# Attention values in key halves over two PSUM banks, turns behind scores, low parts of the sums on GpSimd

## The chip, the cores and the metric

The kernel runs on one core of a Trainium2 chip. The metric is device time in microseconds; the median of three runs of the kernel before is 915.81 us (915.44 to 916.83).

## What is computed

A decoder layer on x (2 x 2048 rows of 512 features): linear self-attention, cross-attention to 154 context rows a batch with 16 heads of 32, and a gated feed-forward, each followed by a layer norm.

```python
x = _layernorm(x + _L0_attn_ref(x, w_qkv, b_qkv, w_o, b_o))          # no softmax: folds into one 512x512 matrix a batch
x = _layernorm(x + _L0_xattn_ref(x, ctx_1024, ctx_1024, mask, ...))
#   scores = q @ k.T / sqrt(32); masked; softmax over 154 keys; out = attn @ v; out @ W_o.T + b_o
x = _layernorm(x + _L0_ffn_ref(x, W_r, W_k, W_v, mu_r, mu_k))
#   xr, xk = blends of x and the row before; sigmoid(xr @ W_r.T) * (relu(xk @ W_k.T) ** 2 @ W_v.T)
```

## The kernel before, in words

Everything is f32. A large product is made of three passes of f32r parts (`three_pass`, L91): high x high, high x low, low x high. So each operand is split: ScalarE writes the high part, VectorE or GpSimd subtracts it to get the low part. The small products of attention and the transposes ("turns") are plain f32.

`prologue` (L117) sums x into a Gram matrix for each batch, makes the keys (`kt`) and values of the context and places the values in the halves and pieces that attention wants (`placements`, DMAs from `v_raw` to `v_first` and `v_rest`), and folds batch 0's self-attention into the matrix `m`.

`layers` (L610) goes over 16 groups of 256 rows (`GT`), two tiles t = 0, 1 of 128 rows. The order of each engine's work is written out by hand, in one program for each engine, and overlapped: in round n TensorE does cross-attention of group n, the first product and q of group a = n + 1, the output product and x2 turns of f = n - 1, and the feed-forward of e = n - 2. Rounds 0 and 1 also fold batch 1. LAST = 15. Semaphores (`Flag`) tie the engines; a `wait_ge` holds everything behind it on its engine.

Cross-attention of a group goes in four head groups g of four heads:
- `scores(n, g)` (L1641): q times keys, 32-row positions, into four banks.
- `masked_min` (VectorE, L1150) adds the mask and takes the row minimum; `exponentials` (ScalarE, L813); `weigh` (GpSimd, L1431) divides by the row sum: `row_inv`, then the keys 128 to 153 into `rest`, then the first 128 into `weight`, whose columns are ordered by key half and head.
- `transposes(n, g, t)` (L1654) turns the weights into the bank `t_bank`; `take_turned` and `take_rest` (ScalarE) copy them to `prob_t`.
- `values(n, g)` (L1671): 24 products, each 64 rows of the array by 32 columns, for three pieces (keys 0 to 63, 64 to 127, the rest), two t and four heads. All pieces of one head and t are summed in PSUM in one row half (`side_of`), in columns 256 to 383 of the two banks `rv_bank` and `t_bank`.
- `o_high` (ScalarE, L833) and `o_low` (VectorE, L1165) read that sum from PSUM and write `o_t_hi` and `o_t_lo`. The next `transposes` waits for `ot_lo`, since it writes a bank that they read; so does the second x2 turn (L1718). `o_product` (L1690), one round later, waits for all four.

x1 turns (`x1_turn`, L1618) need the normalised x1 and a free dense bank; x2 turns go into `t_bank`. `x1t_high` (ScalarE) and `x1t_low` (VectorE) split what is turned. `store` and the loads of x and masks stand in SP's queue.

## Time and profile before

| | |
|---|---|
| median of 3 runs | 915.81 us |
| the profiled execution | 914.96 us, of which the span of instructions is 912.9 us |
| TensorE busy | 896.7 us, 98% |
| VectorE busy | 695.6 us, 76% |
| ScalarE busy | 556.5 us, 61% |
| GpSimd busy | 521.8 us, 57% |
| TensorE's granted clock | 0.998 of full |

Each time in the rows further down is from this one execution. PE is TensorE, DVE VectorE, ACT ScalarE, POOL GpSimd. A row of the timeline gives the start, the length and the instruction; what stands in brackets behind it is the idle time of the engine before it and what ended that. Instructions of one engine overlap a little at their ends, so a row can start before the one ahead has ended.

### The profile page before, as it was taken

What the parts mean: (1) busy time and instruction counts of PE and PEld (TensorE: products, weight loads), DVE (VectorE), ACT (ScalarE), POOL (GpSimd) and SP (SyncE); (2) the same over time, 40 slices, a digit from 0 to 9 for tenths busy, and PEclk for the clock granted to TensorE, in tenths of its full rate; (3) what the DMA queues carried; (4) which work ended last, traced back from release to release, by engine and by line L of the source; (5) the groups of instructions that cost most, each with busy time, mean ns of one, the idle gap of its engine ahead of it and who ended that gap; (6) DMA issues with size and microseconds to landing.
All of it is one profiled execution on the core that took longest, in us unless ns stands there. A gap on an engine that the chain in (4) does not pass through costs nothing.

```text
span 912.9 us, 23290 instructions
## 1 busy us (share of the span) xinstructions
PE 896.7 (98%) x8774; PEld 749.0 (82%) x8774; DVE 695.6 (76%) x1994; ACT 556.5 (61%) x1667; POOL 521.8 (57%) x505
## 2 busy tenths in 40 slices
PE   8999999999999999999999999999999999999997
PEld 7867766787788888888878888888888888888886
DVE  6688566578877878787877878787877777787775
ACT  7555236858675756575856666666665757575631
POOL 1045015759666666666675757566676767665420
PEclk9999999999999999999999999999999999999999
DMA  8792020113000001012101010101010100100001
GB/s 296 245 271 58 24 94 2 43 36 136 9 25 31 25 25 31 24 32 82 32 24 32 24 32 25 32 25 32 25 32 24 31 26 12 44 2 24 2 24 46
DMA packets 32332, 46.54 MB, mean 51 GB/s; under 512 B 3806, under 2 KB 16606, under 8 KB 32094
## 3 DMA queue, kind: packets, MB, share of 16 engines
q1 hardware_dynamic: 28622, 37.99, 12.8%
q10 hardware_dynamic: 3600, 7.08, 2.3%
q8 instruction: 70, 1.15, 0.5%
q14 instruction: 40, 0.33, 0.1%
HBM read 34.10 MB, written 9.70 MB: 48 GB/s over the span
## 4 chain that ended last, share of the span: by engine, by line
PE 75%; DVE 4%; POOL 4%; issue 4%; ACT 1%; POOLq 0%; ACTq 0%
PE dense L92 19%; PE dense L94 17%; PE dense L93 17%; PE turned L1664 5%; PE turned L1686 5%; PE scores L1650 4%; PE dense L1540 2%; PE turned L1668 1%; PE turned L1540 1%; POOL row_inv L1442 1%; POOL weight L1450 1%; PE scores L1546 1%; DVE mix_k_raw L1204 1%; PE dense L1557 0%; POOL prob_rest L1449 0%
## 5 line engine op out<-in xcount | busy, mean ns | idle before, releaser
L1442 POOL TENSOR_TENSOR row_inv<-row_sum,minus_one 128x4 f32<-128x4 f32 x128 | 152.6, 1192 | 190.1 <-ACT prob L818 190.0
L818 ACT ACTIVATE prob<-prob,row_min 128x154 f32<-128x154 f32 x512 | 209.6, 416 | 39.8 <-DVE row_min L1160 39.8
L1450 POOL TENSOR_TENSOR weight<-prob,row_inv 128x512 f32<-128x512 f32 x128 | 148.0, 1156 | 0.0
L1160 DVE CUSTOM_DVE_ANT_0 prob<-scores,mask_add 128x154 f32<-128x154 f32 x512 | 127.8, 312 | 4.0 <-PE scores L1650 3.7
L826 ACT ACTIVATE prob_t<-turned 128x512 f32<-128x512 f32 x128 | 76.0, 594 | 84.6 <-PE turned L1664 83.8
L818 ACT ACTIVATION_READ_ACCUMULATOR prob<-prob,row_min 128x1 f32 x512 | 98.3, 192 | 0.0
L1664 PE MATMUL turned<-ident,weight 128*128 128x128 f32 x512 | 76.9, 272 | 3.4 <-DVE o_t_lo L1167 3.0
L1664 PEld LDWEIGHTS turned<-ident,weight 128*128 128x128 f32 x512 | 61.2, 139 | 17.9 <-issue 6.3
L92 PE MATMUL dense<-mix_k_hi,ffn_wk_hi 128*128 128x256 f32 x256 | 75.3, 294 | 0.0
L92 PE MATMUL dense<-xt_hi,cross_wq_hi 128*128 128x256 f32 x256 | 75.2, 294 | 0.0
L94 PE MATMUL dense<-mix_k_hi,ffn_wk_lo 128*128 128x256 f32 x256 | 72.3, 283 | 0.0
L93 PE MATMUL dense<-mix_k_lo,ffn_wk_hi 128*128 128x256 f32 x256 | 72.3, 283 | 0.0
L94 PE MATMUL dense<-xt_hi,cross_wq_lo 128*128 128x256 f32 x256 | 72.3, 283 | 0.0
L93 PE MATMUL dense<-xt_lo,cross_wq_hi 128*128 128x256 f32 x256 | 72.3, 282 | 0.0
L837 ACT ACTIVATE o_t_hi<-turned 128x256 fp32r<-128x256 f32 x64 | 24.3, 380 | 64.7 <-PE turned L1686 64.0
L1460 POOL TENSOR_TENSOR x<-x,cross_bo_row 128x1024 f32<-128x1024 f32 x16 | 38.6, 2412 | 40.8 <-PE dense L1540 40.8
L1128 DVE TENSOR_SCALAR x<-x,moments,rstd 128x512 f32<-128x512 f32 x64 | 32.1, 544 | 35.1 <-POOL rstd L1429 35.1
L1449 POOL TENSOR_TENSOR prob_rest<-prob,row_inv 128x104 f32<-128x104 f32 x128 | 51.5, 402 | 10.0
L1454 POOL TENSOR_TENSOR mix_r_lo<-mix_r_raw,mix_r_hi 128x1024 fp32r<-128x1024 f32 x16 | 42.2, 2636 | 24.9 <-ACT mix_r_hi L867 24.9
L92 PE MATMUL dense<-m_hi,xt_hi 128*128 128x512 f32 x128 | 52.3, 408 | 1.4 <-DVE x L1173 1.1
L92 PE MATMUL dense<-cross_wo_hi,o_t_hi 128*128 128x512 f32 x128 | 53.1, 415 | 0.0
L92 PE MATMUL dense<-ffn_wv_hi,k_act_hi 128*128 128x512 f32 (+1 forms) x124 | 52.2, 421 | 0.0
(276 smaller groups left out, 2684.7 us busy)
## 6 DMA issues: line engine op xcount, KB each, us to landing
x_rows<-x_rows SPq DMA_DIRECT2D x32, 256.0 KB, 4.6
xt_raw<-x_cols SPq DMA_DIRECT2D x16, 512.0 KB, 3.8
out<-gate_then_y SPq DMA_DIRECT2D x15, 512.0 KB, 2.8
mask_in<-mask SPq DMA_DIRECT2D x16, 154.0 KB, 2.3
cross_wv<-cross_wv SPq DMA_DIRECT2D x2, 512.0 KB, 6.6
cross_wk<-cross_wk SPq DMA_DIRECT2D x1, 1024.0 KB, 9.3
self_wv<-self_wv ACTq DMA_DIRECT2D x1, 1024.0 KB, 7.3
self_wk<-self_wk ACTq DMA_DIRECT2D x1, 1024.0 KB, 9.6
```

The lines of the kernel that those rows point to most:

```text
L92: pe.matmul(out, sta[0], mov[0], start=first, stop=False, skip_group_check=True)
L93: pe.matmul(out, sta[0], mov[1], start=False, stop=False, skip_group_check=True)
L94: return pe.matmul(out, sta[1], mov[0], start=False, stop=last, skip_group_check=True)
L818: m = act.activation(keys, keys, ACT.Exp, bias=row_min[:, buf, t, h:h + 1], scale=-1.0, accum_out=row_sum[:, buf, t, h:h + 1])
L826: act.activation(pt[:, 0:HPG, t * P:(t + 1) * P], t_bank[:].rearrange("p (c n) -> p c n", c=HPG), ACT.Copy).then_inc(*t_out.up)
L1160: m = dve.tensor_tensor_reduce(exp_slot(n, u)[:, i * CTX:(i + 1) * CTX], s_bank[:, h, t * CTX:(t + 1) * CTX], mask_add[n % 2][:, t, :], -S ...
L1442: pool.tensor_tensor(row_inv[:, buf, t, :], row_sum[:, buf, t, :], minus_one[:], ALU.pow).then_inc(*p_inv.up)
L1449: pool.tensor_tensor(after, late, inv_late, ALU.mult)
L1450: pool.tensor_tensor(first, early, inv_early, ALU.mult).then_inc(*p_norm.up)
L1454: pool.tensor_tensor(mix["r"][1][:], mixed["r"][:], f32(mix["r"][0][:]), ALU.subtract).then_inc(*mix_lo["r"].up)
L1664: m = pe.transpose(t_bank[:, i * P:(i + 1) * P], weight_slot(n, u)[:, i * P:(i + 1) * P], ident[:])
L1686: m = pe.matmul(value[h * DK:(h + 1) * DK, t, :], sta, pt[rows, block, t * P:(t + 1) * P], start=(piece == 0), stop=(piece == PIECES), ski ...
```

## The change

- `values`: 8 products of 64 x 32 positions with 256 moving columns (both t at once) for the first 128 keys, half of the keys in each row half of the array, and 8 of 128 columns for the rest. Row half 0 sums into `rv_bank`, row half 1 into `t_bank`, columns 256 to 511. The weights keep the order of heads (`place_of`), so `v_first` has one copy of each row in place of two.
- The two partial sums are added by VectorE (`o_take`, a reduce over two values) into `o_t_raw` in SBUF. `o_high` reads that. `o_low` reads it too, on GpSimd in the rounds and on VectorE in the last round. `transposes` and the second x2 turn wait for `ot_sum`, `o_product` for `ot_lo` as before.
- `prob0` and `prob1` hold both tiles of a head group and are weighed in place; `masked_min` waits for no `p_norm` and `weigh` for no `t_mm`. The difference of the blends has a tile of its own. There is one `mask_in`, so `load_mask(n)` waits for `mask_ok(n - 1)`.
- Order on TensorE: the first turn of g = 1 and of g = 3 stands directly behind `scores`; x2's second turn stands ahead of x1's; products are split less. The other engines' orders follow; ScalarE does `exponentials(a, 0, ...)` ahead of `take_turned(n, 3, 1)`.
- The prologue has fewer placements and its `take_sums(1)` does not wait for them.

```diff
 def place_of(h, t):
-    return h // SIDES * SIDES + side_of(h, t)
+    return (h + t * SIDES) % HPG
...
-    rest_t, value = rv_bank[:, 0:GT], psum[1][:, :, GT:GT + P]
+    rest_t, value = rv_bank[:, 0:GT], psum[1][:, :, GT:2 * GT]
...
             def o_high(n, g):
-                act.wait_ge(*pv_mm.at(n, g + 1))
-                if n:
-                    act.wait_ge(*o_mm.at(n - 1))
-                act.activation(by_t(ot_hi[:, g, :]), value, ACT.Copy).then_inc(*ot_hi_ok.up)
+                act.wait_ge(*ot_sum.at(n, g + 1))
+                act.activation(ot_hi[:, g, :], ot_raw[:, g, :], ACT.Copy).then_inc(*ot_hi_ok.up)
...
+            def o_take(n, g):
+                dve.wait_ge(*pv_mm.at(n, g + 1))
+                if n:
+                    dve.wait_ge(*o_mm.at(n - 1))
+                dve.tensor_reduce(ot_raw[:, g, :], value.rearrange("p s n -> p n s"), mybir.AxisListType.X, ALU.add).then_inc(*ot_sum.up)
...
+            def o_low(n, g):
+                pool.wait_ge(*ot_hi_ok.at(n, g + 1))
+                pool.tensor_tensor(ot_lo[:, g, :], ot_raw[:, g, :], f32(ot_hi[:, g, :]), ALU.subtract).then_inc(*ot_lo_ok.up)
...
                 elif n + g:
-                    pe.wait_ge(*ot_lo_ok.at(n, g))
+                    pe.wait_ge(*ot_sum.at(n, g))
...
-                for piece in range(PIECES + 1):
-                    for t in range(TPG):
-                        for h in range(HPG):
-                            rows = slice(side_of(h, t) * SIDE_ROWS, (side_of(h, t) + 1) * SIDE_ROWS)
...
+                for side in range(SIDES):
+                    rows = slice(side * SIDE_ROWS, (side + 1) * SIDE_ROWS)
+                    for h in range(HPG):
+                        cols = slice((g * HPG + h) * DK, (g * HPG + h + 1) * DK)
+                        pe.matmul(value[h * DK:(h + 1) * DK, side, :], v_first[rows, b, cols], pt[rows, h, :],
+                                  start=True, stop=False, skip_group_check=True)
+                for t in range(TPG):
+                    for h in range(HPG):
+                        side = place_of(h, t) // SIDES
+                        rows = slice(side * SIDE_ROWS, (side + 1) * SIDE_ROWS)
+                        m = pe.matmul(value[h * DK:(h + 1) * DK, side, t * P:(t + 1) * P],
+                                      v_rest[rows, b, g, h * DK:(h + 1) * DK], pt[rows, HPG, t * P:(t + 1) * P],
+                                      start=False, stop=True, skip_group_check=True)
...
                 scores(n, 2)
+                transposes(n, 1, 0)
                 y_product(a, 1)
-                transposes(n, 1, 0)
+                transposes(n, 1, 1)
                 r_product(e, 0)
-                transposes(n, 1, 1)
...
                 scores(n, 3)
+                x2_turn(f, 1)
                 x1_turn(a, 1)
-                x2_turn(f, 1)
...
                 scores(a, 0)
+                transposes(n, 3, 0)
                 v_product(e, 0)
-                transposes(n, 3, 0)
-                v_product(e, 1, early)
                 transposes(n, 3, 1)
-                v_product(e, 1, late_half)
+                v_product(e, 1)
                 values(n, 3)
...
                 if live(e - 1):
                     scale(3, e - 1)
+                if live(f):
+                    o_low(f, 3)
                 if a >= 2:
                     x_low(a)
```

TensorE behind `scores(n, 2)` of a settled round, before (`weight` is what the turn of g = 1 reads; its row stands 12 products further on):

```order
L1650 MATMUL scores<-kt,q 128x154 [waits s_min,q_out]
L1650 MATMUL scores<-kt,q 128x154 x7
L92 MATMUL dense<-m_hi,xt_hi 128x512 [waits o_sum]
L93 MATMUL dense<-m_lo,xt_hi 128x512
L94 MATMUL dense<-m_hi,xt_lo 128x512
```

and now:

```order
L1656 MATMUL scores<-kt,q 128x154 [waits s_min,q_out]
L1656 MATMUL scores<-kt,q 128x154 x7
L1671 MATMUL turned<-ident,prob_91 128x128 [waits ot_sum,p_norm]
L1671 MATMUL turned<-ident,prob_91 128x128 x3
L90 MATMUL dense<-m_hi,xt_hi 128x512 [waits o_sum]
```

The turn has moved ahead of the whole y product and waits for `ot_sum`.

TensorE behind `scores(n, 3)`, before (x_1_88 is x1, x_1_98 is x2):

```order
L1650 MATMUL scores<-kt,q 128x154 [waits s_min,q_out]
L1650 MATMUL scores<-kt,q 128x154 x7
L1540 MATMUL dense<-ident,x_1_88 128x128 [waits r_out,ln1]
L1540 MATMUL dense<-ident,x_1_88 128x128 x3
L1540 MATMUL turned<-ident,x_1_98 128x128 [waits ot_lo,ln2]
```

and now (x_1_99 is x2):

```order
L1656 MATMUL scores<-kt,q 128x154 [waits s_min,q_out]
L1656 MATMUL scores<-kt,q 128x154 x7
L1545 MATMUL turned<-ident,x_1_99 128x128 [waits ot_sum,ln2]
L1545 MATMUL turned<-ident,x_1_99 128x128 x3
L1545 MATMUL dense<-ident,x_1_88 128x128 [waits r_out,ln1]
```

The x2 turn, which waits for the sum of g = 1, is now the first of the two.

GpSimd at the turn from round to round, before (from the second tile of g = 0):

```order
L1442 TENSOR_TENSOR row_inv<-row_sum,minus_one 128x4 [waits p_exp]
L1449 TENSOR_TENSOR prob_rest_92<-prob,row_inv 128x2x2x26 [waits t_mm,rest_mm,p_inv]
L1450 TENSOR_TENSOR weight<-prob,row_inv 128x4x2x64
L1429 TENSOR_TENSOR rstd_1449<-var_1448,neg_half 128x2 [waits ln3,var3]
L1422 TENSOR_TENSOR xt_lo<-xt_raw,xt_hi 128x1024 [waits x_hi_ok]
```

and now:

```order
L1436 TENSOR_TENSOR row_inv<-row_sum,minus_one 128x4 [waits p_exp]
L1441 TENSOR_TENSOR prob_rest_92<-prob_90,row_inv 128x4x26 [waits rest_mm,p_inv]
L1442 TENSOR_TENSOR prob_90<-prob_90,row_inv 128x4x128
L1428 TENSOR_TENSOR rstd_1441<-var_1440,neg_half 128x2 [waits ln3,var3]
L1447 TENSOR_TENSOR o_t_lo<-o_t_raw,o_t_hi 128x256 [waits ot_hi]
L1421 TENSOR_TENSOR xt_lo<-xt_raw,xt_hi 128x1024 [waits x_hi_ok]
```

The low part of g = 3 stands behind two tiles' weights and an `rstd`.

## Rows read from the trace of the kernel before

**Rows 1.** Busy time by stretch: us of each engine (instructions), granted clock, DMA share, GB/s.
```profile
288.50:335.50 47.00, 47.00 (x506) 40.07 (x506) 36.73 (x115) 30.15 (x97) 31.39 (x31) 1.00 0.09 28
```

**Rows 2.** Timeline, VectorE and TensorE, rounds 0 to 2: start, us, instruction, idle before.
```profile
159.53 0.41 DVE L1167 TENSOR_TENSOR o_t_lo<-turned,o_t_hi 128x256 fp32r<-128x256 f32 x1
...
160.09 0.63 PE L1664 MATMUL turned<-ident,weight 128*128 128x128 f32 x4 [2.00 <-DVE o_t_lo L1167]
...
211.71 0.63 PE L1664 MATMUL turned<-ident,weight 128*128 128x128 f32 x4 [0.98 <-DVE o_t_lo L1167]
...
235.11 0.47 PE L92 MATMUL dense<-ffn_wr_hi,mix_r_hi 128*128 128x512 f32 x1 [0.92 <-DVE x L1136]
...
245.43 0.63 PE L1540 MATMUL turned<-ident,x 128*128 128x128 f32 x4 [0.81 <-DVE o_t_lo L1167]
```

**Rows 3.** Timeline of TensorE, round 6, values(6,0) to the turn of g = 1.
```profile
419.34 0.67 PE L1686 MATMUL turned<-prob_t,v_first 64*32 64x128 f32 x32
419.80 0.48 PE L1686 MATMUL turned<-prob_t,v_rest 64*32 64x128 f32 x16
420.21 0.81 PE L1650 MATMUL scores<-kt,q 32*128 32x154 f32 x16
420.94 0.50 PE L92 MATMUL dense<-m_hi,xt_hi 128*128 128x512 f32 x1
...
423.80 0.60 PE L1664 MATMUL turned<-ident,weight 128*128 128x128 f32 x4
```

**Rows 4.** Chain that ended last: start us, us, what.
```profile
118.65 3.43 PE scores L1546 x8
```

**Rows 5.** Groups by line and form: busy us, mean ns; idle before, releaser.
```profile
L1167 DVE TENSOR_TENSOR o_t_lo<-turned,o_t_hi 128x256 fp32r<-128x256 f32 x64 | 27.0, 422 | 23.9 <-ACT o_t_hi L837 23.9
...
L1115 DVE BATCH_NORM_STATS2 stats<-x 128x6 f32<-128x512 f32 x64 | 44.4, 695 | 2.2
...
L1460 POOL TENSOR_TENSOR x<-x,cross_bo_row 128x1024 f32<-128x1024 f32 x16 | 38.6, 2412 | 40.8 <-PE dense L1540 40.8
```

**Rows 6.** Timeline of TensorE, round 6, behind scores(6,3).
```profile
433.00 0.66 PE L1540 MATMUL dense<-ident,x 128*128 128x128 f32 x4
433.49 0.60 PE L1540 MATMUL turned<-ident,x 128*128 128x128 f32 x4
```

**Rows 7.** Timeline of ScalarE, round 6.
```profile
420.33 0.38 ACT L837 ACTIVATE o_t_hi<-turned 128x256 fp32r<-128x256 f32 x1 [4.20 <-PE turned L1686]
...
451.45 0.42 ACT L818 ACTIVATE prob<-prob,row_min 128x154 f32<-128x154 f32 x1
```

**Rows 8.** Timeline of VectorE, round 6.
```profile
420.63 1.00 DVE L1128 TENSOR_SCALAR x<-x,moments,rstd 128x512 f32<-128x512 f32 x2 [1.66 <-POOL rstd L1429]
...
432.18 0.69 DVE L1147 TENSOR_TENSOR xt_lo<-dense,xt_hi 128x512 fp32r<-128x512 f32 x1 [2.90 <-ACT xt_hi L802]
432.80 0.42 DVE L1167 TENSOR_TENSOR o_t_lo<-turned,o_t_hi 128x256 fp32r<-128x256 f32 x1
...
446.27 0.42 DVE L1167 TENSOR_TENSOR o_t_lo<-turned,o_t_hi 128x256 fp32r<-128x256 f32 x1 [2.04 <-ACT o_t_hi L837]
```

**Rows 9.** Timeline of all engines, start of round 6.
```profile
405.19 0.67 PE L1686 MATMUL turned<-prob_t,v_first 64*32 64x128 f32 x32
...
408.10 0.42 DVE L1167 TENSOR_TENSOR o_t_lo<-turned,o_t_hi 128x256 fp32r<-128x256 f32 x1
...
410.13 0.48 PE L92 MATMUL dense<-cross_wo_hi,o_t_hi 128*128 128x512 f32 x1
...
411.46 0.70 POOL L1429 TENSOR_TENSOR rstd<-var,neg_half 128x2 f32<-128x2 f32 x1
...
412.60 3.08 DVE L1128 TENSOR_SCALAR gate_then_y<-gate_then_y,moments,rstd 128x512 f32<-128x512 f32 x2
```

**Rows 10.** Timeline of VectorE and TensorE, last round.
```profile
841.06 0.67 PE L1686 MATMUL turned<-prob_t,v_first 64*32 64x128 f32 x32
...
843.40 0.41 DVE L1167 TENSOR_TENSOR o_t_lo<-turned,o_t_hi 128x256 fp32r<-128x256 f32 x1
```

474 lines of the change are left out of this document (228 added, 246 removed).

## The prediction

> **What bounds the kernel.** I read the busy shares and slices of the page first: TensorE is busy 98% of the span of 912.9 us, at the full granted clock (2.4 GHz) in every slice. The windows say it more sharply [rows 1]: in one round TensorE is busy 47.00 of 47.00 us, VectorE 36.73, ScalarE 30.15, GpSimd 31.39. So in a settled round (one of n = 2 to 14, 47.0 us each) TensorE never waits, and the other engines live in its shadow. TensorE's few waits lie in the rounds before [rows 2], and one of 1.1 us at the turn of the batch. What the change can win is time in which TensorE works; what it can lose is any wait that TensorE has not got now. I went through TensorE's timeline of round 6 with those of VectorE, ScalarE and GpSimd beside it, measuring from the start of each `values` block, called v.
>
> **Values in two banks.** Today a block is 24 products of 128 columns, 48 passes since f32 runs as two: 419.34 to 420.21, 0.87 us [rows 3]. The change makes 8 products of 256 columns and 8 of 128, 32 passes. A full f32 pass of 512 columns takes 3.43/8 = 0.43 us [rows 4], so 0.107 for 128 columns and 0.214 for 256. Eight positions run together, so today 6 x 0.107 = 0.64 us stand in a row, and then 2 x 0.214 + 2 x 0.107 = 0.64: the same. What can shrink is the rest, 0.87 - 0.64 = 0.23. If that is all fixed, nothing is won; if it is per pass, 4 of 6 shares stay and 0.08 is won. I take 0.055, nearer to the second, since the last 16 passes are slow (0.41 us for 16, 0.46 for the 32 before), though part of that is the change of shape to `scores`. 64 blocks: **-3.5 us** (0 to -5). All 32 first passes of today run in 0.46 us, four bursts of 0.115, with both row halves writing one bank. The Trainium skill ("TensorEngine Tiling (Array Packing)", "Gotcha 1: PSUM Pressure") says that different row tiles cannot use one PSUM bank at a time. By it today's halves would take turns, 8 x 0.107 = 0.86 us for those 32, and separate banks would save much more; the trace disagrees, and my sum has no such term.
>
> **The sum out of two banks.** VectorE gets `o_take`, a reduce over 2 x 256 values in PSUM, and gives up `o_low` (0.42). No reduce is in the trace. By its output it would take the 0.42 of `o_t_lo`, by its 512 inputs the 0.69 of `bn_stats` [rows 5]. I take 0.69, since `bn_stats` writes only 6 values and pays for the 512 it reads. That is 0.27 more, 64 times, on an engine with 10 us free a round: nothing by itself. What counts is when it is done, because TensorE's next write to the turned bank waits for it (`ot_sum`).
>
> **Turns behind scores.** The first turn of g = 1 and of g = 3 moves from behind a product (2.86 us, 420.94 to 423.80 [rows 3]) to right behind `scores`. On TensorE itself the first turn behind `scores` takes 0.49 (433.00 to 433.49 [rows 6]), a tenth more than within a product, and a product broken up once less gives nearly that back: 28 places, +0.3 us at most. But the cover is gone. For g = 1 `scores` is over at v + 0.815 + 0.735 = v + 1.55. A reader of the finished sums starts today at 420.33, v + 0.99 [rows 7], so at v + 0.93 with the shorter block; VectorE is idle there (1.66 us before 420.63 [rows 8]) and is done at v + 1.62. From a VectorE end to TensorE's start it is 0.15 (159.94 to 160.09 [rows 2]). The turn starts at v + 1.77: a new wait of 0.22. For g = 3 VectorE is idle too, from 444.23 [rows 8], v + 0.5, and the wait is the same. 2 x 0.22 x 13 rounds: **+5.7 us** (0 if the reduce takes 0.42).
>
> **The dearest place: x2 before x1 behind scores(n,3).** Today the x1 turn goes first (433.00), and the x2 turn, which waits for the sums of g = 1, follows at 433.49 [rows 6], just after `o_t_lo` ends at 433.22 [rows 8]. Now x2 comes first and wants to start at v + 1.55 = 432.95. But on VectorE `o_take(n,1)` still stands behind `x1t_low(a,0)`, which waits for ScalarE and starts at 432.18 [rows 8] whatever the change does. So the reduce starts at 432.80, ends at 433.49, and TensorE goes on at 433.64. A wait of 0.69 in 13 rounds: **+9.0 us** (+5.5 if the reduce takes 0.42). That such a wait reaches TensorE is seen in round 2, where a late `o_t_lo` holds this very turn for 0.81 [rows 2].
>
> **Low parts on GpSimd.** GpSimd adds 1024 values in 2.41 us [rows 5], so 256 in about 0.65, four times a round, out of 15.6 us free. Only the last one has a reader near: `o_product(f,0)` waits for `ot_lo(f,3)`. Today that is done at 408.52 and wanted at 410.13, with v = 405.19, v + 4.94 [rows 9]. Then: VectorE is free of `v_finish` at 408.10, v + 2.91; reduce until 3.60, high part on ScalarE (0.38 [rows 7]) until 4.02, GpSimd until 4.75, TensorE 4.90; wanted 4.88. What stands in GpSimd's queue ahead decides: today `weigh(n,0,1)` ends at 411.46 [rows 9], 1.4 us too late. But the change puts ScalarE's exponentials of the next tile ahead of the last turned copies, about 3.6 us sooner than today's 451.45 [rows 7], and that work of GpSimd's with them, to about v + 2.7. So **0 us** (0 to +0.5 a round). GpSimd's later low parts have over 1 us of slack by the same walk. One thing gets better: the two normalises at 412.60, 3.08 us in place of 1.00 [rows 8, 9] because GpSimd's `xt_lo` runs, find it over sooner.
>
> **Rounds outside the settled ones.** Round 0: the wait of 2.00 at 160.09 goes, since a fold and a product now stand ahead of that turn; but the turn before loses the fold that covered it (2 x 0.43) and has a reduce ahead (0.27 and some tenths): -0.7. Round 1: two waits of 0.2, and the turn at 211.71 (wait 0.98) has half a product, 1.4 us, moved behind it and a reduce ahead: +2.0. Round 2: `y_finish(3,0)` moves up, the wait of 0.92 at 235.11 goes: -0.9 [rows 2]. Last round: no y product stands between `o_product` and `values`, so VectorE comes to `o_take(15,0)` only at 843.40 [rows 10], TensorE goes on at 844.24; with v = 841.06 it wants to at 842.61: +1.4 after some slack. Tail: a reduce in the chain to `o_product(15,0)`, +0.5. Prologue: TensorE waits for no placement, so fewer of them give 0. One mask buffer makes SP wait for the mask, made in the middle of the round; the x load behind it waits for the q product, later, anyway: 0. Together **+2.3 us**.
>
> **Sum.** -3.5 + 0.3 + 5.7 + 9.0 + 0 + 2.3 = +13.8 us. The profiled execution took 914.96 us, 0.85 below the median 915.81 of the runs. 914.96 + 13.8 = 928.8, against the median 929.6. I say **929**.
>
> **Rivals.**
> A, *the reduce costs what it writes*, 0.42: the waits of the turns vanish and x2 keeps 0.42: -3.5 + 0.3 + 0 + 5.5 + 1.2 = +3.5, **919**. For it: `o_t_lo` writes 256 in 0.42. Against: `bn_stats`.
> B, *the block goes by its instructions* (the other side): 48 passes in 0.87 us are 18 ns each, 32 take 0.58, 0.29 saved in 64 blocks: -18.6 in place of -3.5, in all -1; with the cheap reduce too, -12: **903 to 914**. With the waits as worked out it decides from 0.27 saved a block. For it: the slow last 16 passes. Against: bursts of 0.115 are the pass rate of 0.107 already. If the banks did matter, it would be in this case.
> C, *GpSimd is late*: the low part of g = 3 finds GpSimd busy or stretched, by another low part and an `rstd` (0.65 + 0.70 [rows 9]) at most, and `o_product` waits 0.4 to 1.3 us in 13 rounds: +5 to +17, **934 to 946**. For it: the margin worked out is nil, and 3.08 in place of 1.00 [rows 8, 9] shows what the two engines do to each other. Against: 31 of 47 us are in use. The Trainium skill ("SBUF — State Buffer", "Who interferes with whom") says that VectorE, in a two-port mode or with two SBUF inputs, and GpSimd take one shared port pair for a whole instruction and block each other; by it each of the four new GpSimd instructions could hold VectorE up for its length.
> D, *the new order does not bind*: the waits stay under the gain, no change, 915.
>
> **Chances.** Forecast (924 to 934) 0.50; A 0.16; B 0.12; C 0.18; D 0.04. Runs of this kernel can tell 0.2% (1.8 us) from no change. Faster: B and little else, 0.13. Same 0.05. Slower 0.82. The range leaves out B and the far end of C: 916 to 943.
>
> **What would show it.** In a settled round of about 47.9 us, some 1.1 us of TensorE's waits on VectorE's reduce, the longest before the x2 turn; a values block of 0.81; a reduce of 0.69; no wait for GpSimd ahead of `o_product`. A reduce of 0.42, a block under 0.6 or rounds of 47.0 would prove me wrong, each in its own term; rounds over 48.5 with waits at `o_product` would be C.

## The result, and the profile after

The changed kernel takes **950.4 us** (median of 4 runs, 948.85 to 952.64), the kernel before 916.13 beside it: 1.038 times as long (95% interval 1.035 to 1.040), 34 us slower. I had said 929 (916 to 943). The profiled execution took 952.64 us, span 950.9, which is 38.0 more than the 912.9 of before; the comparison of the traces is against these 38. It is the slowest of the four runs of the change, so the traces differ by more than the medians do.

Lines of the page of the changed kernel (the page lists the groups by source line and names what a group waited for): busy times, TensorE's granted clock in 40 slices, the chain that ended last by engine, and the groups of the reduce and of GpSimd's low part (busy us, mean ns, idle before).

```profile
PE 902.5 (95%) x7750; PEld 743.4 (78%) x7750; DVE 721.1 (76%) x2003; ACT 549.0 (58%) x1663; POOL 567.6 (60%) x564
PEclk9999999998999999999999999999999999999999
PE 47%; DVE 24%; issue 9%; POOL 5%; ACT 4%; POOLq 0%; DVEq 0%; ACTq 0%
L1447 POOL TENSOR_TENSOR o_t_lo<-o_t_raw,o_t_hi 128x256 fp32r<-128x256 f32 x59 | 59.0, 999 | 6.3 <-ACT o_t_hi L815 6.3
L1146 DVE TENSOR_REDUCE o_t_raw<-turned 128x256 f32<-128x512 f32 x64 | 43.9, 685 | 23.6 <-PE turned L1694 23.5
```

The reduce is 0.685 as forecast, the low part 1.00 on average where I had worked out 0.65. The third line is the chain that ended last, by engine: a quarter of it now runs over VectorE (the same line before: PE 75%, DVE 4%). Slice 10 has a granted clock below full.

One settled round by the windows view (columns as in [rows 1]). TensorE was busy 47.00 of 47.00 before; now it is busy 47.05 of 48.88, so 1.8 us of every settled round are waits.

```profile
374.14:423.02 48.88, 47.05 (x441) 39.40 (x440) 38.62 (x115) 29.67 (x97) 34.65 (x35) 1.00 0.08 26
```

TensorE's timeline of that round (start, us, instruction, idle before and who ended it), the rows that answer to [rows 3] and [rows 6]:

```profile
374.14 0.66 PE L1688 MATMUL turned<-prob_t,v_first 64*32 64x256 f32 x16
374.60 0.42 PE L1694 MATMUL turned<-prob_t,v_rest 64*32 64x128 f32 x16
374.96 0.81 PE L1656 MATMUL scores<-kt,q 32*128 32x154 f32 x16
...
378.62 0.60 PE L1671 MATMUL turned<-ident,prob 128*128 128x128 f32 x4
379.52 0.50 PE L90 MATMUL dense<-cross_wo_hi,o_t_hi 128*128 128x512 f32 x1 [0.31 <-POOL o_t_lo L1447]
...
389.54 0.81 PE L1656 MATMUL scores<-kt,q 32*128 32x154 f32 x16
390.56 0.63 PE L1671 MATMUL turned<-ident,prob 128*128 128x128 f32 x4 [0.22 <-DVE o_t_raw L1146]
...
401.82 0.81 PE L1656 MATMUL scores<-kt,q 32*128 32x154 f32 x16
403.24 0.63 PE L1545 MATMUL turned<-ident,x 128*128 128x128 f32 x4 [0.61 <-DVE o_t_raw L1146]
...
414.71 0.81 PE L1656 MATMUL scores<-kt,q 32*128 32x154 f32 x16
416.21 0.63 PE L1671 MATMUL turned<-ident,prob 128*128 128x128 f32 x4 [0.69 <-DVE o_t_raw L1146]
```

The values block is 374.14 to 374.96, 0.82 by these rows (0.811 is the median of the 64 blocks, against 0.868 before). Four waits stand in the round. From start to start, with before in brackets: turn to `o_product` 0.91 (0.35), +0.55; `scores` to the turn of g = 1 1.02 (0.74), +0.28; `scores(n,3)` with the x2 and x1 turns 2.24 (1.58), +0.66; `scores(a,0)` to the turn of g = 3 1.50 (0.74), +0.76. Together +2.25. The four blocks give back 0.22. The round is 1.87 longer (48.88 against 47.01), so another 0.16 is given back, which I put down to products that are broken up once less; it is not traced.

Where the 38 us lie, each row from the start of one `values(n,3)` to the next, the last one to the end of TensorE's work:

| stretch | before | after | more |
|---|---|---|---|
| into round 1 | 41.3 | 45.1 | 3.8 |
| into round 2 | 48.9 | 57.6 | 8.8 |
| 12 settled rounds | 565.5 | 586.3 | 20.8 |
| last round | 37.5 | 40.7 | 3.2 |
| behind the last `values` | 39.2 | 40.8 | 1.6 |

Among the 12 is the round at the turn of the batch, 48.31 before with a wait of 1.12 that is gone after; there the change costs only 0.6, which is most of why 20.8 is less than 12 times 1.87.

**Why the sums are late.** VectorE and then GpSimd in the same round:

```profile
375.05 1.41 DVE L1210 SCALAR_TENSOR_TENSOR gate_then_y<-gate_then_y,x 128x512 f32<-128x512 f32 x1
377.52 0.69 DVE L1146 TENSOR_REDUCE o_t_raw<-turned 128x256 f32<-128x512 f32 x1
...
401.80 0.69 DVE L1127 TENSOR_TENSOR xt_lo<-dense,xt_hi 128x512 fp32r<-128x512 f32 x1 [2.76 <-ACT xt_hi L782]
402.41 0.68 DVE L1146 TENSOR_REDUCE o_t_raw<-turned 128x256 f32<-128x512 f32 x1
405.63 2.25 DVE L1173 TENSOR_TENSOR diff<-x_t 128x1024 f32<-128x1024 f32 x1
407.92 2.03 DVE L1183 SCALAR_TENSOR_TENSOR mix_k_raw<-diff,cols,x_t 128x256 f32<-128x256 f32 x4
410.48 2.17 DVE L1183 SCALAR_TENSOR_TENSOR mix_r_raw<-diff,cols,x_t 128x256 f32<-128x256 f32 x4
413.41 2.06 DVE L1189 TENSOR_TENSOR mix_k_lo<-mix_k_raw,mix_k_hi 128x1024 fp32r<-128x1024 f32 x1
415.39 0.68 DVE L1146 TENSOR_REDUCE o_t_raw<-turned 128x256 f32<-128x512 f32 x1
```

```profile
374.87 1.04 POOL L1442 TENSOR_TENSOR prob<-prob,row_inv 128x512 f32<-128x512 f32 x1
378.74 0.73 POOL L1447 TENSOR_TENSOR o_t_lo<-o_t_raw,o_t_hi 128x256 fp32r<-128x256 f32 x1 [0.36 <-ACT o_t_hi L815]
...
404.38 2.41 POOL L1457 TENSOR_TENSOR x<-x,cross_bo_row 128x1024 f32<-128x1024 f32 x1 [3.86 <-PE dense L1545]
406.74 1.74 POOL L1447 TENSOR_TENSOR o_t_lo<-o_t_raw,o_t_hi 128x256 fp32r<-128x256 f32 x1
```

These rows show a relay. The difference starts at 405.63, while GpSimd adds the bias until 406.79; it ends at 407.88, 1.1 us after that. GpSimd's low part, begun at 406.74, ends 0.6 after the difference. Each does most of its own time (1.28 and 0.74 where they hardly meet) only once the other has finished. The same stands at 375.05: the second step of `v_finish` takes 1.41 beside GpSimd's weighing, against 0.69 where nothing meets it (over all 30 the mean went from 0.75 to 1.07). With the turns back behind the products (e2 and e5 below) the weighing ends 0.37 earlier in the round, the step takes 1.05, and `o_product` comes 0.36 sooner after v. The reduce for g = 2 then waits for the whole row of work, until 415.39, though its sums were there at 414.83 or so (0.93 after its values block started, at 413.90).

**Round 2** has the dearest waits. TensorE, GpSimd and ScalarE:

```profile
226.97 0.79 PE L90 MATMUL dense<-cross_wo_hi,o_t_hi 128*128 128x512 f32 x1 [2.88 <-POOL o_t_lo L1447]
255.70 0.63 PE L1545 MATMUL turned<-ident,x 128*128 128x128 f32 x4 [1.97 <-DVE o_t_raw L1146]
```

```profile
222.38 0.41 ACT L815 ACTIVATE o_t_hi<-o_t_raw 128x256 fp32r<-128x256 f32 x1
223.33 1.01 POOL L1436 TENSOR_TENSOR row_inv<-row_sum,minus_one 128x4 f32<-128x4 f32 x1
225.73 1.18 POOL L1447 TENSOR_TENSOR o_t_lo<-o_t_raw,o_t_hi 128x256 fp32r<-128x256 f32 x1
```

The high part is done at 222.8, but in GpSimd's queue the weighing of both tiles (`weigh(2,0,0)` and `weigh(2,0,1)`) stands ahead of the low part. And the wait costs more than itself (windows view; the last three columns are granted clock, DMA share, GB/s):

```profile
224.00:226.00 2.00, 0.09 (x1) 0.00 (x0) 1.05 (x2) 1.75 (x6) 1.92 (x4) 1.00 1.01 385
226.00:228.00 2.00, 1.03 (x3) 0.84 (x4) 0.33 (x1) 1.23 (x7) 2.00 (x2) 0.56 0.11 43
228.00:230.00 2.00, 2.00 (x6) 1.61 (x5) 0.00 (x0) 0.00 (x0) 2.00 (x2) 0.50 0.69 230
230.00:232.00 2.00, 2.00 (x6) 1.52 (x6) 0.00 (x0) 0.00 (x0) 1.56 (x3) 0.50 0.76 294
232.00:234.00 2.00, 2.00 (x12) 1.67 (x11) 1.44 (x3) 0.72 (x2) 0.00 (x0) 0.74 0.00 0
```

After standing nearly idle for two microseconds TensorE is granted half its clock, 1.2 of 2.4 GHz, for some six: the shares missing from 1.00 sum to 0.44 + 0.50 + 0.50 + 0.26 in four windows of 2 us, up to 3.4 us of work lost beside the 2.88 of the wait. The two other long waits of these rounds end likewise: behind the 2.08 before `o_product` in round 1 the windows from 180 to 186 show 0.96, 0.50 and 0.68, 1.7 us lost; behind the 1.97 in round 2 those from 256 to 262 show 0.74, 0.50 and 0.91, 1.7 us. So up to 6.8 of the 38 us are the clock's in this execution.

### The profile page after: what moved, and what is told of

The parts are those of the page before. It is cut to its first block, busy times and chain, and to the rows that moved or that the text cites. A ratio compares the mean times of both kernels' runs of the same rounds, so it can differ in the third digit from the quotient of the medians.

```text
span 950.9 us, 21187 instructions
## 1 busy us (share of the span) xinstructions
PE 902.5 (95%) x7750; PEld 743.4 (78%) x7750; DVE 721.1 (76%) x2003; ACT 549.0 (58%) x1663; POOL 567.6 (60%) x564
## 3 DMA queue, kind: packets, MB, share of 16 engines
q8 instruction: 62, 1.02, 0.4%
## 4 chain that ended last, share of the span: by engine, by line
PE 47%; DVE 24%; issue 9%; POOL 5%; ACT 4%; POOLq 0%; DVEq 0%; ACTq 0%
PE dense L90 13%; PE dense L92 12%; PE dense L91 12%; DVE o_t_raw L1146 4%; PE turned L1671 4%; DVE mix_r_raw L1183 3%; DVE diff L1173 3%; DVE mix_k_lo L1189 3%; DVE gate_then_y L1210 2%; DVE mix_k_raw L1183 2%; DVE stats L1095 2%; ACT xt_hi L782 2%; POOL o_t_lo L1447 1%; PE turned L1545 1%; DVE gate_then_y L1207 1%
## 5 line engine op out<-in xcount | busy, mean ns | idle before, releaser
L1436 POOL TENSOR_TENSOR row_inv<-row_sum,minus_one 128x4 f32<-128x4 f32 x128 | 142.0, 1109 | 138.5 <-ACT prob L798 138.4
L1442 POOL TENSOR_TENSOR prob<-prob,row_inv 128x512 f32<-128x512 f32 x128 | 141.5, 1106 | 0.0
L1671 PE MATMUL turned<-ident,prob 128*128 128x128 f32 x512 | 78.1, 275 | 16.1 <-DVE o_t_raw L1146 15.3
L1671 PEld LDWEIGHTS turned<-ident,prob 128*128 128x128 f32 x512 | 59.7, 141 | 30.5 <-issue 18.8
L815 ACT ACTIVATE o_t_hi<-o_t_raw 128x256 fp32r<-128x256 f32 x64 | 26.5, 414 | 75.8 <-DVE o_t_raw L1146 75.8
L1441 POOL TENSOR_TENSOR prob_rest<-prob,row_inv 128x104 f32<-128x104 f32 x128 | 57.0, 445 | 10.0
L1447 POOL TENSOR_TENSOR o_t_lo<-o_t_raw,o_t_hi 128x256 fp32r<-128x256 f32 x59 | 59.0, 999 | 6.3 <-ACT o_t_hi L815 6.3
L1146 DVE TENSOR_REDUCE o_t_raw<-turned 128x256 f32<-128x512 f32 x64 | 43.9, 685 | 23.6 <-PE turned L1694 23.5
L1428 POOL TENSOR_TENSOR rstd<-var,neg_half 128x2 f32<-128x2 f32 x47 | 32.7, 696 | 47.6 <-DVE var L1102 44.6
L1451 POOL TENSOR_TENSOR mix_r_lo<-mix_r_raw,mix_r_hi 128x1024 fp32r<-128x1024 f32 x16 | 45.4, 2836 | 22.5 <-ACT mix_r_hi L845 22.5
```

The costliest lines, as they stand in the source:

```text
L1146: dve.tensor_reduce(ot_raw[:, g, :], value.rearrange("p s n -> p n s"), mybir.AxisListType.X, ALU.add).then_inc(*ot_sum.up)
L1436: pool.tensor_tensor(row_inv[:, buf, t, :], row_sum[:, buf, t, :], minus_one[:], ALU.pow).then_inc(*p_inv.up)
L1441: pool.tensor_tensor(after, keys[:, :, P:CTX], inv.broadcast_to([P, HPG, CTX - P]), ALU.mult)
L1442: pool.tensor_tensor(keys[:, :, 0:P], keys[:, :, 0:P], inv.broadcast_to([P, HPG, P]), ALU.mult).then_inc(*p_norm.up)
L1447: pool.tensor_tensor(ot_lo[:, g, :], ot_raw[:, g, :], f32(ot_hi[:, g, :]), ALU.subtract).then_inc(*ot_lo_ok.up)
L1671: m = pe.transpose(t_bank[:, h * P:(h + 1) * P], prob[g % 2][:, t, i * CTX:i * CTX + P], ident[:])
```

## The experiments

"The change" below is the changed kernel whole; each experiment starts from it unless said otherwise.

### e1: x1 turn first again

```diff
                 scores(n, 3)
-                x2_turn(f, 1)
                 x1_turn(a, 1)
+                x2_turn(f, 1)
```

(ScalarE's two copies are exchanged likewise; rounds 2 to 14, as in e2 and e5.)

> The changed kernel with one pair of turns exchanged in the rounds 2 to 14: behind scores(n,3) the x1 turn goes first again, then the x2 turn. In the changed kernel the x2 turn stands 0.61 us idle there in every settled round, until VectorE's reduce of g = 1 ends. Theory (the wait is for the reduce, and 0.46 us of other work fits into it): the wait shrinks to about 0.2, the settled round goes from 48.84 to 48.4, and the kernel from 950.4 to about 945. Rival (the wait is given back at the next place, since VectorE sets the pace of the round): round stays 48.8, kernel stays at 950.

Measured **938.4** (938.18 to 938.87), round 47.93: 12 us less, more than twice the 5.4 that I expected. VectorE and GpSimd at the same place:

```profile
400.41 1.28 DVE L1173 TENSOR_TENSOR diff<-x_t 128x1024 f32<-128x1024 f32 x1
...
409.36 0.69 DVE L1146 TENSOR_REDUCE o_t_raw<-turned 128x256 f32<-128x512 f32 x1
```

```profile
398.20 2.41 POOL L1457 TENSOR_TENSOR x<-x,cross_bo_row 128x1024 f32<-128x1024 f32 x1 [2.78 <-PE dense L1545]
```

The bias addition waits for the x1 turn. With that turn first, it is over at 400.6, just as the difference begins: 1.28 in place of 2.25. So the order of two turns of 0.4 us costs twice: 0.44 at the turns themselves, and 0.47 of the 0.69 before the turn of g = 3, by way of the collision that it sets up. Outside the settled rounds the stretches into rounds 1 and 2 are 1.5 and 1.9 shorter in this trace; the clock stays at 1.00 behind the same wait in round 1 and behind that at the x2 turn in round 2 (1.38 here), so part of the 12 us is the clock's.

### e2: the turns of g = 1 and g = 3 behind the products again

```diff
-                transposes(n, 1, 0)
                 y_product(a, 1)
+                transposes(n, 1, 0)
...
-                transposes(n, 3, 0)
                 v_product(e, 0)
+                transposes(n, 3, 0)
```

(The second turns and ScalarE's copies move back with them.)

> The changed kernel with the first turns of g = 1 and g = 3 put back behind the y and the v product in the rounds 2 to 14 (on TensorE, and the copies that follow them on ScalarE). Theory (the turns lost their cover; 0.28 + 0.75 us of waits in each round stand there now): both waits go, the round is 47.8, the kernel 937. Rival 1 (the wait before the turn of g = 3, which I had put at 0.22 and which is 0.69, is VectorE's load and comes back at the values block): round 48.3 to 48.8, kernel 944 to 950. Rival 2 (no wait for reduces matters, GpSimd is the bound): the wait before o_product grows from 0.31 to over 1.

Measured **936.6** (933.30 to 938.27), round 47.60; most of the settled rounds have no wait over 0.1 but that of the x2 turn (0.61). The theory holds.

### e5: both pairs back in the settled rounds

The edits of e1 and e2 together.

> The changed kernel with both pairs of turns put back in the rounds 2 to 14 (x1 before x2 behind scores(n,3); the turns of g = 1 and g = 3 behind the products). Values in two banks, the reduce and the low parts on GpSimd stay. Theory (the whole loss of the settled rounds is the order of the turns, and what stays is the gain of the two banks, 0.055 in 4 blocks of a round): round 46.8, below the 47.01 of before, no wait over 0.2 in it, kernel 924, all that is left over 916 lying in the rounds 0 to 2 and the last. Rival (the low parts on GpSimd cost on their own): a wait before o_product stays, round 47.1 to 47.4, kernel 927 to 931.

Measured **930.6** (929.63 to 931.35), round 47.15. Between theory and rival: the order explains 1.7 of the 1.87 us, but the round stays over the 47.01 of before. From start to start two delays are left, 0.19 before `o_product` (0.54 for 0.35) and 0.22 at the x1 and x2 turns (1.80 for 1.59). e1 and e2 together save less than their sum (0.95 + 1.28), since both contain the 0.47.

### e7: one bank read

```diff
-                dve.tensor_reduce(ot_raw[:, g, :], value.rearrange("p s n -> p n s"), mybir.AxisListType.X, ALU.add)
+                dve.tensor_copy(ot_raw[:, g, :], value[:, 0, :])
```

The second bank's values are left out of the sum.

> The changed kernel with a copy of 256 values of the first bank in place of the reduce over both; the values of the second bank are left out of the sum. Theory A (the reduce of 0.69 costs by its 512 inputs, and the waits behind it by its length): the copy takes 0.42, the waits before the turns of g = 1 and g = 3 lose 0.27 each, that before the x2 turn 0.27 too, the round is 48.0 and the kernel 939 to 941. Theory B (most of the loss hangs on when VectorE gets to it, not on its length): waits shrink by under 0.1 each, kernel 946 to 950.

Measured **934.5** (933.58 to 935.68), round 47.79, 1.05 less: the 0.27 by which the copy (0.418 on average) is shorter than the reduce, once at each of the four places. `o_product` comes 0.29 sooner after v, the turns of g = 1, x2 and g = 3 lose 0.27 each. Theory A, somewhat stronger, since I had left `o_product` out.

### e3 and e4: sums moved, the wrong way

e3 has all low parts on VectorE:

```diff
                 o_take(n, 1)
                 masked_min(n, 3, 0)
+                o_low(n, 1)
                 masked_min(n, 3, 1)
                 x1t_low(a, 1)
```

(and the other g likewise, none on GpSimd in the rounds).

> The changed kernel with all low parts of the sums on VectorE, none on GpSimd; the order of TensorE is untouched. Theory A (what GpSimd holds up is VectorE: while o_t_lo runs there, VectorE's difference of x2 takes 2.25 us where it took 1.58, and everything behind it is late): the difference goes back to about 1.6, the wait of 0.69 before the turn of g = 3 shrinks to under 0.4 though VectorE got 1.7 us more work, the long waits of rounds 1 and 2 before o_product (2.08 and 2.88 us) go under 1, TensorE keeps its full granted clock in round 2, and the kernel takes 930 to 936. Theory B (only the place in GpSimd's queue counts): the waits before o_product go, 0.31 in 13 rounds and 4 us in rounds 1 and 2 with the lost clock, 3 us more, but the wait before the turn of g = 3 stays at 0.69 or grows: 938 to 942. Theory C (VectorE is the bound by now): slower than 950.

Measured **963.9** (963.04 to 964.10), round 50.29: none of my theories as I argued them, C only by its sign. VectorE's rows:

```profile
402.03 1.75 DVE L1150 TENSOR_TENSOR o_t_lo<-o_t_raw,o_t_hi 128x256 fp32r<-128x256 f32 x1 [1.29 <-ACT o_t_hi L815]
...
404.65 0.68 DVE L1127 TENSOR_TENSOR xt_lo<-dense,xt_hi 128x512 fp32r<-128x512 f32 x1
```

VectorE stood 1.29 us for a high part that ScalarE makes behind the x1 copy, then 1.75 beside GpSimd, and `xt_lo`, queued behind, held the q product 1.13 us in this round. It is a verdict on the place, not on the engine: e11 has the low parts on VectorE at other places, and no wait.

e4, on VectorE alone:

```diff
+                o_take(f, 3)
                 if live(e - 1):
                     v_finish(e - 1, 1)
-                o_take(f, 3)
...
-                k_mix_low(f)
                 o_take(n, 2)
+                k_mix_low(f)
```

> The changed kernel with VectorE's reduce moved ahead of one neighbour at two places in the rounds 2 to 14: the reduce of g = 3 ahead of v_finish(e-1,1), the reduce of g = 2 ahead of k_mix_low(f). Nothing else moves. Theory (the reduce stands behind work that GpSimd stretches: v_finish's second step takes 1.41 us in place of 0.69, k_mix_low 2.06): the wait before o_product(f,0) goes (0.31) and that before the turn of g = 3 falls from 0.69 to 0.2, the round is 48.0 and the kernel 938 to 940. Rival (the low parts come late for GpSimd's own sake): the wait before o_product stays at 0.3. Rival (k_mix_low comes late for k_product of the next round): a new wait of 0.5 or more before k_product(e,0), kernel 945 to 950.

Measured **965.3** (961.60 to 966.31), round 49.75. `o_product` waited 0.85. GpSimd's rows say why:

```profile
380.90 0.70 POOL L1428 TENSOR_TENSOR rstd<-var,neg_half 128x2 f32<-128x2 f32 x1 [1.77 <-DVE var L1102]
381.57 0.73 POOL L1447 TENSOR_TENSOR o_t_lo<-o_t_raw,o_t_hi 128x256 fp32r<-128x256 f32 x1
```

The reduce was early (377.43 to 378.12), but the low part stood behind an `rstd` that waits for the `v_finish` I had delayed. The second edit delayed the row minima of the next tile, and with them ScalarE's exponentials, which stand ahead of the last turned copies: a new wait of 0.76 before `values(n,3)`. One half of the theory held: the wait before the turn of g = 3 is 0.22.

### e6: GpSimd's queue in rounds 0 and 1

```diff
                 weigh(a, 0, 0)
+                if n in (0, 1):
+                    o_low(n, 3)
                 weigh(a, 0, 1)
```

> The changed kernel with only two instructions moved, both on GpSimd: the low part of g = 3 of the rounds 0 and 1 goes ahead of weigh(a,0,1) instead of behind it. In the changed kernel o_product waits 2.08 us for it in round 1 and 2.88 us in round 2, and after the second wait TensorE's granted clock is 0.50 from about 227 to 233 us. Theory (place in GpSimd's queue, and the clock lost for the wait): both waits shrink to under 0.8, the granted clock stays 1.00 there, and the kernel takes 942 to 944, of which 3 us are the clock's. Rival (the clock falls whatever this wait does): 946 to 947, with a stretch of granted clock 0.50 at the same place.

Measured **943.0** (941.80 to 943.45), 7.4 less. No wait over 0.5 is left before `o_product` in rounds 1 and 2, and where the clock was halved it now reads (windows view, same stretch of the program):

```profile
220.00:222.00 2.00, 1.99 (x9) 1.63 (x10) 1.15 (x2) 1.75 (x6) 1.92 (x3) 1.00 0.96 368
222.00:224.00 2.00, 2.00 (x13) 1.71 (x12) 1.77 (x3) 1.59 (x7) 2.00 (x2) 1.00 0.05 19
```

The waits themselves were 2.08 + 2.88 = 5.0; the stretches into rounds 1 and 2 became 3.9 and 6.6 shorter in the traces, 10.5 in all; the granted clock is 1.00 throughout both. The theory holds.

### e14: one low part moved behind the weighing

```diff
-                    o_low(n, 1)
                     weigh(n, 3, 0)
                 if live(n):
                     weigh(n, 3, 1)
+                    o_low(n, 1)
```

> The changed kernel with one instruction a round moved: GpSimd's low part of g = 1 goes behind weigh(n,3,1); nobody waits for it before the next round. In the changed kernel it takes 1.74 us there, while VectorE's difference of x2 takes 2.25 us, against 1.30 in e1 where the two hardly met. Theory (each holds the other up, and what is late behind the difference is ScalarE's turned copy for the values block of g = 2, 0.35, and the reduce before the turn of g = 3, 0.47 of its 0.69): the difference takes 1.3 to 1.6, both waits shrink, the settled round is 48.0 to 48.3 and the kernel 940 to 944. Rival (it is the bias addition and row_inv of GpSimd that stretch the difference, and the late x2 turn itself that delays): the difference stays over 2.0, round 48.7 to 48.8, kernel 948 to 951.

Measured **944.1** (943.04 to 945.47), round 48.4: the time of the theory, with the difference of the rival:

```profile
401.82 2.26 DVE L1173 TENSOR_TENSOR diff<-x_t 128x1024 f32<-128x1024 f32 x1
404.11 1.78 DVE L1183 SCALAR_TENSOR_TENSOR mix_k_raw<-diff,cols,x_t 128x256 f32<-128x256 f32 x4
406.42 1.85 DVE L1183 SCALAR_TENSOR_TENSOR mix_r_raw<-diff,cols,x_t 128x256 f32<-128x256 f32 x4
```

The bias addition stretches the difference; what the low part stretched were the two blends behind it (2.03 and 2.17 in the change). They are 0.6 us shorter together, and 0.47 went from the wait before the turn of g = 3 (0.69 to 0.22). So the 0.47 takes both collisions. In e1 the difference is short and the blends are as long as in the change (2.02 and 2.17); here it is the other way round; in both the reduce begins 1.0 us after the values block starts, which is as soon as its sums are there, in place of 1.5 in the change.

### e8 to e15: what the two banks are worth

e8: TensorE's and ScalarE's order of before in the rounds 1 to 15, and the edit of e6. What stays is values in two banks, the reduce and low parts on GpSimd.

> The changed kernel with TensorE's and ScalarE's order of before in the rounds 1 to 15, and the two low parts of the rounds 0 and 1 early on GpSimd. What stays of the change: values in two banks, the reduce, low parts on GpSimd, one mask buffer. Theory (all that was lost is order; the two banks are worth 3.5 us): the rounds 1 and 2 take 41.5 and 49, the settled ones 46.8, the last 38, the kernel 912 to 914, 0.2 to 0.4% under the one before. Rival 1 (the reduce and GpSimd cost a few waits in the rounds outside the settled ones in any order): 916 to 920. Rival 2 (the settled rounds keep a wait for GpSimd): 920 to 925.

Measured **920.9** (920.64 to 921.97), 1.0051 of before (1.0038 to 1.0063): rival 2, with the 47.17 us round of e5, and 4.7 us lost in the last round, where on VectorE the low part of group 14 stood behind `k_square` and the reduce of g = 2 behind `v_finish`: waits of 1.31 and 1.90, and behind the second the clock at half, 1.7 us.

e9: on top of e8 the sums come early (in the rounds 2 to 14 as in e10; the last round's too):

```diff
+                o_take(f, 3)
                 if live(e - 1):
                     v_finish(e - 1, 1)
-                o_take(f, 3)
...
+                o_take(n, 1)
                 x1t_low(a, 0)
-                o_take(n, 1)
```

(VectorE; on GpSimd `o_low(f, 3)` goes ahead of `scale(3, e - 1)`.)

> The kernel e8_all_back with the sums taken and split earlier: on VectorE the reduce of g = 3 ahead of v_finish(e-1,1) and that of g = 1 ahead of x1t_low(a,0) (in round 2 the split of ffn_wv goes behind them), on GpSimd the low part of g = 3 ahead of rstd, and the last round's reduces and low parts ahead of k_square and v_finish. TensorE's order is that of e8. Theory (a settled round of e8, 47.17, has two waits left, about 0.19 before o_product and 0.20 before the x2 turn, each on the way reduce, high part, low part; the four blocks give 0.22; the last round lost 1.4 and 1.9 us to the same chain): settled round 46.8, last round and tail 4 us less, kernel 909 to 912, 0.5% under the one before. Rival (TensorE is not held by this chain but by another engine that comes right behind): round 47.0 to 47.2, kernel 915 to 919.

Measured **917.0** (914.75 to 918.96), 1.0013 (1.0003 to 1.0022). The settled round is as the theory said, and TensorE idles nowhere in it:

```profile
374.00:420.77 46.77, 46.77 (x442) 39.37 (x441) 36.23 (x116) 29.98 (x97) 33.54 (x35) 1.00 0.09 27
```

But round 2 and the tail took it back: the moved split of `ffn_wv` made `q_product` wait 2.44, and `o_product` of the last group waited 1.91, each with 1.7 us of lost clock behind it.

e10: the same early sums under the change's own order of TensorE.

> The changed kernel with TensorE's order untouched, and the same early places for the settled rounds as e9: the reduce of g = 3 ahead of v_finish, that of g = 1 ahead of x1t_low(a,0), GpSimd's low part of g = 3 ahead of rstd. e4, which moved the first of them and k_mix_low, was 15 us slower than the change; in its trace the low part stood behind the rstd of the delayed v_finish, and ScalarE's turned copies behind exponentials that k_mix_low delayed. Theory (the order of TensorE can be borne if the reduces come in time): wait before o_product gone, before the x2 turn 0.2, before the turn of g = 3 0.22, round 47.5 to 47.7, kernel 932 to 936. Rival (GpSimd's queue delays the low part whatever stands first): o_product waits 0.3 or more, round 48.3 or more, kernel 943 or more.

Measured **941.5** (939.57 to 942.56), round 47.9, between theory and rival. The wait before `o_product` is gone, and those before the turns of g = 1 and x2 are 0.22 each: these turns right behind `scores` keep the reduce's length over the cover of `scores`. But before the turn of g = 3 TensorE still waits 0.70. VectorE's rows of that round (the values block of g = 2 starts at 411.63):

```profile
403.83 1.78 DVE L1173 TENSOR_TENSOR diff<-x_t 128x1024 f32<-128x1024 f32 x1
405.65 2.04 DVE L1183 SCALAR_TENSOR_TENSOR mix_k_raw<-diff,cols,x_t 128x256 f32<-128x256 f32 x4
413.13 0.68 DVE L1146 TENSOR_REDUCE o_t_raw<-turned 128x256 f32<-128x512 f32 x1
```

Both collisions are still there, and the reduce begins 1.5 after the block as in the change. This is the loss that e10 was to mend and did not.

e11: e9 with the low parts on VectorE, each behind work that gives ScalarE time:

```diff
                 x1t_low(a, 1)
+                o_low(n, 1)
```

> The kernel e9_sums_early with all low parts on VectorE (behind one row minimum or more, so that ScalarE's high part is there). Theory A (on GpSimd the low parts stand where they stretch VectorE's instructions with two inputs in SBUF; off the path either way): within 1 us of e9. Theory B (VectorE, now with 2.9 us more a round, is late at a turn): a wait of 0.2 to 0.5 in each settled round, kernel 3 to 7 us over e9. Theory C (GpSimd was the hidden cost): 2 us or more under e9.

Measured **915.0** (913.81 to 915.77), 0.9989 (0.9981 to 0.9998); settled rounds equal to e9's (561.8 us for the 12 against 562.1). So in settled rounds GpSimd's low parts cost nothing once nobody waits. The traces differ by 2.5 us, 1.9 of them behind the last `values`: there e9's `o_product` waits 1.91 and the windows from 872 to 878 show a granted clock of 0.92, 0.50 and 0.73, 1.7 us lost; e11's waits 1.72 and its clock stays at 1.00. That is one execution of each; that the medians differ for the same reason is not shown.

e12 and e13: e9 and e11 with two places mended:

```diff
+                if n == 2:
+                    weight_low_part("ffn_wv", 0, 1)
                 normalise(1, a, x1[a % 2])
...
                 x1t_low(a, 0)
+                if n == 2:
+                    weight_low_part("ffn_wv", 2, 3)
...
+            o_take(LAST, 3)
             k_square(LAST - 1, 0)
-            o_take(LAST, 3)
```

> The kernel e9_sums_early with the two places mended at which its trace still loses time: in round 2 VectorE splits ffn_wv in quarters, two in its idle time before the normalising of x1 and two behind x1t_low(a,0) (e9 had all 2.85 us in one piece ahead of k_square, and q_product waited 2.44 us), and in the last round the reduce of g = 3 stands ahead of k_square and its low part ahead of k_low (o_product of the last tile waited 1.91 us). Low parts of the rounds stay on GpSimd. Theory (the two banks are worth 0.24 us a round and nothing else is lost): round 2 under 49.5, the last round and what follows 1.5 to 3 us less, kernel 911 to 913, 0.3 to 0.5% under the one before. Rival (the granted clock and the fixed part of those rounds take it back): 915 to 917.

> The kernel e11_low_vector_back with the same two edits as e12. Theory A (GpSimd's low parts cost nothing once no one waits for them): within 1 us of e12; the 2 us between e9 and e11 lay in the clock of the last rounds. Theory C (they cost something): 2 us or more under e12, so 909 to 911.

Measured **916.6** (915.17 to 917.16) and **914.9** (913.72 to 915.71), 1.0009 (1.0000 to 1.0017) and 0.9991 (0.9982 to 1.0000) of before: the rival of e12, and hardly less than e9 and e11. In round 2 `q_product` still waited 2.3 us. VectorE and GpSimd in e12:

```profile
245.37 3.49 DVE L1055 TENSOR_TENSOR ffn_wv_lo<-ffn_wv_raw,ffn_wv_hi 128x512 fp32r<-128x512 f32 x2
```

```profile
245.45 2.86 POOL L1466 TENSOR_TENSOR x<-x,cross_bo_row 128x1024 f32<-128x1024 f32 x1 [0.77 <-PE dense L1556]
```

Two quarters took 3.49 there. The two before them took 1.83.

e15: e13 with those two quarters at other places, the last round's first three low parts on GpSimd, idle there, and one ScalarE instruction of the last round put back in its order:

```diff
+                    weight_low_part("ffn_wv", 2)
                 o_take(n, 1)
...
                 x1t_low(a, 1)
+                if n == 2:
+                    weight_low_part("ffn_wv", 3)
...
                 for t in range(TPG):
                     weigh(LAST, g, t)
+                o_low(LAST, g - 2)
+            o_low(LAST, 2)
```

> The kernel e13_fill_low_vector with its two last losses mended. In round 2 the third and the fourth quarter of ffn_wv (the fourth took 2.9 us beside GpSimd's bias addition of 2.86, and q_product waited 2.33 us for what stood behind) go ahead of the reduce of g = 1 and behind x1t_low(a,1). In the last round, where VectorE is 1.3 us later than in the kernel before and GpSimd idle, the low parts of g = 0 to 2 go to GpSimd, and ScalarE's relu ahead of the high part again. Theory (two banks are worth 0.24 us in each settled round, 3.1 in all, once nothing else is lost): round 2 at 49.5, tail 39.5 to 40.2, kernel 911.5 to 913, 0.3 to 0.4% under the one before. Rival (the time of one place comes back at the next): 914 to 915.

Measured **911.6** (910.72 to 911.93) against 916.4: ratio 0.995 (0.9936 to 0.9963), 0.5% faster than the kernel before and 4% faster than the change. Round 2 is 48.4, 3.2 less than in e13: the wait for `q_product` fell from 2.33 to 0.65, and the 1.7 us of clock that e13 lost behind it are not lost. Settled rounds are 46.77 to 46.98, the last 37.3. By the traces e15 is 3.3 us under the kernel before: 3.7 in the 12 settled rounds, 0.6 in round 2 and the last, and 1.0 is lost behind the last `values`. Of the 3.7, 1.4 come from the round at the turn of the batch (46.89 for 48.31), where the wait of 1.12 is gone; so not all of the 0.5% is the two banks'. Two lines of its page, busy times and the chain that ended last:

```profile
PE 893.0 (98%) x7750; PEld 738.5 (81%) x7750; DVE 706.2 (78%) x2062; ACT 552.6 (61%) x1663; POOL 514.3 (57%) x508
PE 75%; DVE 7%; issue 3%; ACT 1%; POOL 1%; POOLq 0%; ACTq 0%
```

## Why the prediction was wrong

The sign was right, the size was not: +34 where I had +13.8. By my terms a settled round grew by 0.93 us, and it grew by 1.87; the rest of the kernel was to lose 2.3 and lost 17 in the trace. Point by point.

- **Values in two banks, -3.5 us**: the size was right, 0.811 a block and 46.77 for a round of 47.01 where nothing is in the way (e9). The reason was not. I took a share for each pass that goes, but the first 128 keys take 0.456 in 16 passes and took 0.461 in 32. The whole 0.05 lies in the last 16 passes (0.355 for 0.408), which are as many as before. That the sum came out is luck; why those got faster is open.
- **The sum out of two banks**, 0.69: right (0.685), and e7 shows that its 0.27 over a copy reaches TensorE at four places, where I counted three (`o_product` was missing).
- **Turns behind scores, 2 x 0.22**: right for g = 1 (0.22 idle, +0.28 from start to start). For g = 3 the step that failed is "for g = 3 VectorE is idle too, from 444.23, v + 0.5". I read VectorE's place off the trace of before, but the change moves VectorE as well: the x2 turn makes everything behind it later, and it now meets GpSimd. The reduce begins at 415.39 instead, 1.5 after the block's start. +0.76 in place of 0.22; e1 and e14 take off 0.47 each by ending one of the two collisions, and e10, which ends neither, takes off nothing here.
- **The dearest place, 0.69**: the wait itself was 0.61, so the term was sized right, but it was not the whole price: e1 gives back 0.9 a round. I never asked what a late x2 and x1 turn start: the bias addition on GpSimd and the difference on VectorE, which in the trace of before met only in part (the difference took 1.58 there; [rows 5] showed the addition, and [rows 8, 9] what a meeting does).
- **Low parts on GpSimd, 0 to +0.5**: it was 0.55 in each settled round. My walk had VectorE free of `v_finish` at v + 2.91, by the durations of before. I moved GpSimd's weighing forward to free GpSimd, and did not ask on what of VectorE's it would now lie: the second step of v_finish, 0.69 to 1.41. The reduce began at v + 3.38 and `o_product` at v + 5.38, where 4.88 was wanted. My walk ended at 4.90, with no margin. That was rival C, whose condition I had named "stretched" and whose chance, 0.18, was too low for a margin of nil. The two normalises did get over sooner, as forecast (0.99 for 3.08).
- **Rounds outside the settled ones, +2.3**: the worst term; 17.4 in the table (of which some 2 belong to round 2's share of the settled waits). Into round 1 I had +2.0 and it was +3.8, round 2 -0.9 and +8.8, the last round +1.4 and +3.2, behind it +0.5 and +1.6. I had no term for `o_product` of the rounds 1 and 2 (waits of 2.08 and 2.88), where GpSimd's queue has the weighing ahead of the low part, and none for the clock (up to 6.8 in this execution). I also had nothing for the x2 turn of round 2, which waits 1.97 where it waited 0.81: its reduce stands behind the split of `ffn_wv` (2.29, until 254.36) and `xt_lo`. I walked through GpSimd's queue in one settled round only.

The rule of the Trainium skill ("SBUF — State Buffer", "Who interferes with whom") that I had put behind rival C says that a VectorE instruction with two inputs in SBUF contends with a GpSimd instruction that reads SBUF, and that the lock on the port pair they share is exclusive. The trace agrees but for some tenths: 2.25 for a difference of 1.28, 1.74 for a low part of 0.74, each with 0.1 to 0.2 of its own time done while the other still ran. The same section says that on this chip a reduce never contends; the trace agrees here too, for the longest of the 64 is 0.69, and the one at 415.39 lies whole inside a GpSimd subtraction (`mix_r_lo`, 414.67 to 417.70).

What stays open: why the last 16 passes of a block got faster, and what makes the granted clock fall after one wait and not after another.

## What to carry to other kernels

Before a turn or a low part is moved, walk the change twice: once with the durations of before, and once more with every instruction that has become late or early laid over what the other engine of the shared port does at that moment; where the margin that comes out is nil, count it as lost. Look in the first two and the last round at each queue by itself, since there a wait of some 2 to 3 us was also followed by half the clock, 1.7 to 3.4 us more. And a change that bundles a small gain (0.24 us a round) with a new order should be tried without the order: here the bundle cost 3.8%, the two banks without it still 0.5% (e8), and the gain shows only once the sums are taken before the work that may be late and the places of round 2 and the last round are mended (e15).
